# A four-layer GNN on one core: in the tensor product's edge stage, the eightfold copies of the hidden rows as one transfer each, the edge rows' products behind the next brackets, and TensorE's waits split by pair of chunks

## What is computed

```python
s1, v1 = scalars (16) and vectors (16 x 3) of both end nodes of an edge
w   = relu(emb @ fc1_w1 / sqrt(10)) @ fc1_w2 / sqrt(16)      # 4 matrices of 16 x 8 for each edge
s_t = a1 * (einsum(s1, Wss) + einsum(vdot1, Wvv))
v_t = a1 * (einsum(s1, Wsv) * sh1 + einsum(v1, Wvs))
w2  = relu(emb @ fc2_w1 / sqrt(10)) @ fc2_w2 / sqrt(16)      # 6 matrices of 8 x 8 for each edge
scal, gates, vecs = the same kind of products of s_t, v_t with w2
edge_out = concat([tanh(scal), vecs * tanh(gates)]) * norm
out = segment_sum(edge_out, edge_dst)
```

## Time and profile before

| what | us |
|---|---|
| time before, median of 3 runs | 26026.72 (26022.92 to 26029.44) |
| the profiled execution, its own time | 26033.88 |
| its span, first to last instruction | 26032.1 |
| DVE busy | 15740.5 (60%) |
| PE busy | 14761.0 (57%) |
| POOL busy | 14448.5 (56%) |
| ACT busy | 5279.9 (20%) |

### The profile page before, as it was taken

How to read it: one execution, slowest core, us unless ns; L and a number is a source line. 1 busy time by engine, 2 the same in 40 slices (tenths; PEclk the granted TensorE clock), 3 DMA queues, 4 the chain that set the end, 5 groups by cost and what they waited for, 6 DMA issues and landing times. The chain is left out here.

```text
span 26032.1 us, 473806 instructions
## 1 busy us (share of the span) xinstructions
PE 14761.0 (57%) x105565; PEld 9264.3 (36%) x105566; DVE 15740.5 (60%) x32221; ACT 5279.9 (20%) x13135; POOL 14448.5 (56%) x14298
## 2 busy tenths in 40 slices
PE   7555555567666679972000000005577777777777
PEld 5344444334333368851000000005233333333333
DVE  9666666665556654442111114995777777777777
ACT  4211111111111134421000000000222222222222
POOL 0377777677777744433777777760333333333333
PEclk9655555555555555555555555555899999999999
DMA  2466666533333345412333332221444544444454
GB/s 66 112 172 173 172 173 172 128 68 68 68 68 68 68 119 154 146 51 53 92 92 92 92 92 79 72 65 30 114 117 117 118 118 118 118 118 119 118 119 110
DMA packets 3004699, 2740.20 MB, mean 105 GB/s; under 512 B 1459983, under 2 KB 2366029, under 8 KB 3001618
## 3 DMA queue, kind: packets, MB, share of 16 engines
q1 hardware_dynamic: 2437198, 2308.99, 33.5%
q0 software_dynamic: 412544, 241.53, 6.4%
q10 hardware_dynamic: 153668, 172.93, 2.7%
HBM read 2173.27 MB, written 537.90 MB: 104 GB/s over the span
## 5 line engine op out<-in xcount | busy, mean ns | idle before, releaser
L2571 POOL DMA_INDIRECT rows_x<-x_table,index x3125 | 2961.4, 948 | 5359.1 <-DMA index<-in_src 4596.6
L742 POOL DMA_INDIRECT rows<-split_table,index x3125 | 2999.3, 960 | 1943.2 <-DMA index<-in_src 1008.4
L1624 POOL DMA_INDIRECT rows_dram<-rows,place_now x3125 | 3028.1, 969 | 1489.1 <-issue 951.9
L858 POOL DMA_INDIRECT rows<-x_table,index x3125 | 3282.0, 1050 | 1021.1 <-issue 951.8
L1552 DVE TENSOR_REDUCE rows<-banks 128x108 f32<-128x324 f32 x1250 | 490.3, 434 | 3468.9 <-DMA rows_dram<-rows,place_now 3452.6
L1564 PE MATMUL banks<-row_pieces,hot_turned 128*128 x3125 | 393.6, 290 | 3609.9 <-DMA hot_turned<-turned_dram 3606.6
L2278 DVE TENSOR_TENSOR first<-banks,h 128x768 f32<-128x768 f32 x2500 | 1940.0, 817 | 786.5 <-PE banks L2401 672.1
L2286 DVE TENSOR_TENSOR second<-banks,h 128x768 f32<-128x768 f32 x2500 | 1943.7, 819 | 620.1 <-PE banks L2425 604.1
L550 PE MATMUL banks<-counts,low_turned 128*128 128x98 f32 x6250 | 1783.2, 433 | 82.8 <-ACT counts L538 50.1
L550 PEld LDWEIGHTS banks<-counts,low_turned 128*128 128x128 f32 x6250 | 1591.6, 313 | 205.8 <-issue 175.9
L1564 PEld LDWEIGHTS banks<-row_pieces,hot_turned 128*128 128x128 bf16 x3125 | 251.0, 134 | 3752.5 <-issue 3752.5
(11 more groups left out here) (475 smaller groups left out, 33351.8 us busy)
## 6 DMA issues: line engine op xcount, KB each, us to landing
key_row<-dst_rows SPq DMA_DIRECT2D x1250, 320.0 KB, 3.5
h<-hidden_dram SPq DMA_DIRECT2D x10000, 40.0 KB
acc_moved<-dst_rows SPq DMA_DIRECT2D x625, 320.0 KB
src_row<-in_src_rows SPq DMA_DIRECT2D x625, 320.0 KB
hot_turned<-turned_dram SPq DMA_DIRECT2D x1250, 160.0 KB, 2.2
hot_dram<-onehot SPq DMA_DIRECT2D x625, 160.0 KB
turned_dram<-hot_turned SPq DMA_DIRECT2D x625, 160.0 KB
a_dram<-a ACTq DMA_DIRECT2D x625, 160.0 KB
```

Of the source, the lines that this page charges most:

```text
L742: nc.gpsimd.indirect_dma_start(out=m["rows"][j][:, t * SPLIT:(t + 1) * SPLIT], out_offset=None, in_=m["split_table"], in_offset=bass.Indir ...
L858: nc.gpsimd.indirect_dma_start(out=m["rows"][j][:, t * C2:t * C2 + F], out_offset=None, in_=m["x_table"], in_offset=bass.IndirectOffsetOnA ...
L1624: nc.gpsimd.indirect_dma_start(out=m["rows_dram"], out_offset=bass.IndirectOffsetOnAxis(ap=m["place_now"][j][:, t:t + 1], axis=0), in_=m[" ...
L2571: nc.gpsimd.indirect_dma_start(out=m["rows_x"][j][:, t * F:(t + 1) * F], out_offset=None, in_=m["x_table"], in_offset=bass.IndirectOffsetO ...
```

## The change

It has three parts. `sp_group` loads `h1` and `h2` with one transfer each, whose source repeats the 16 rows eight times (an outermost dimension of 8 with step 0). In `pe_turn` the brackets of the next group's half 0 move ahead of `pe_first_visit`. And in `pe_brackets`, `pe_units`, `pe_spread` and `pe_contract` the wait for VectorE's work moves into the loop over chunks: chunks 0 and 1 wait for the first of its two instructions, chunks 2 and 3 for the second.

```diff
--- before.py
+++ after.py
@@ -2192,10 +2192,9 @@
         if again:
             sp.wait_ge(s["doubled"], ONE + CHUNKS * (g - SLOTS + 1))
         for k, name in enumerate(("h1", "h2")):
-            for u in range(U8):
-                sp.dma_start(m[name][j][K16 * u:K16 * (u + 1), :],
-                             m["hidden_dram"][bass.ds(g, 1), K16 * k:K16 * (k + 1), :].rearrange("g h e -> (g h) e")
-                             ).then_inc(s["hidden_in"][j], 16)
+            sp.dma_start(m[name][j][:, :],
+                         m["hidden_dram"][bass.ds(g, 1), K16 * k:K16 * (k + 1), :].rearrange("g h e -> (g h) e").unsqueeze(0).broadcast_to([U8, K16, T * P])
+                         ).then_inc(s["hidden_in"][j], 16)
         if again:
             sp.wait_ge(s["hot_whole"], ONE + g - SLOTS + 1)
             sp.sem_inc(s["going_sp"], 1)
@@ -2272,7 +2271,7 @@
 
         width = HALVES[half][1]
         if half == 0:
-            dve.wait_ge(s["hidden_in"][j], 32 * U8 * (i + 1))
+            dve.wait_ge(s["hidden_in"][j], 32 * (i + 1))
         for pair in range(2):
             dve.wait_ge(s["brackets"], ONE + CHUNKS * (SLOTS * i + j) + 2 * half + pair + 1)
             nc.vector.tensor_tensor(m["first"][2 * half + pair][:, :].rearrange("p (k e) -> p k e", k=2), bank_pair(4 + 2 * pair, width),
@@ -2394,9 +2393,9 @@
     def pe_brackets(pe, i, j, half):
         g = SLOTS * i + j
         pe.wait_ge(s["flipped"], ONE + 2 * g + half + 1)
-        if not (isinstance(i, int) and g == 0):
-            pe.wait_ge(s["doubled"], ONE + CHUNKS * (g - 1) + 2 * half + 2)
         for chunk in range(CHUNKS):
+            if chunk % 2 == 0 and not (isinstance(i, int) and g == 0):
+                pe.wait_ge(s["doubled"], ONE + CHUNKS * (g - 1) + 2 * half + chunk // 2 + 1)
             rows = slice(32 * ((chunk - 1) % 4), 32 * ((chunk - 1) % 4) + 32)
             mm = nc.tensor.matmul(m["ps"][4 + chunk][:, 0:HALVES[half][1]], m["w_tensor"][rows, chunk * P:(chunk + 1) * P],
                                   m["u_turned"][j % 3][rows, columns(half)], start=True, stop=True)
@@ -2406,10 +2405,11 @@
     def pe_units(pe, i, j, half):
         g = SLOTS * i + j
         width = HALVES[half][1]
-        pe.wait_ge(s["weighted"], ONE + CHUNKS * g + 2 * half + 2)
         if not (isinstance(i, int) and g == 0):
             pe.wait_ge(s["outputs_out"], ONE + 2 * (g - 1) + half + 1)
         for chunk in range(CHUNKS):
+            if chunk % 2 == 0:
+                pe.wait_ge(s["weighted"], ONE + CHUNKS * g + 2 * half + chunk // 2 + 1)
             k = chunk % 2
             mm = nc.tensor.matmul(m["ps"][1][32 * chunk:32 * chunk + 32, 0:width], m["unit_sum"][:, :],
                                   m["first"][2 * half + chunk // 2][:, k * width:(k + 1) * width], start=True, stop=True)
@@ -2418,9 +2418,9 @@
     def pe_spread(pe, i, j, half):
         g = SLOTS * i + j
         pe.wait_ge(s["units_out"], ONE + 2 * g + half + 1)
-        if not (isinstance(i, int) and g == GROUPS - 1 and half == 1):
-            pe.wait_ge(s["weighted"], ONE + CHUNKS * g + 2 * half + 4)
         for chunk in range(CHUNKS):
+            if chunk % 2 == 0 and not (isinstance(i, int) and g == GROUPS - 1 and half == 1):
+                pe.wait_ge(s["weighted"], ONE + CHUNKS * g + 2 * half + chunk // 2 + 3)
             rows = slice(32 * chunk, 32 * chunk + 32)
             mm = nc.tensor.matmul(m["ps"][4 + chunk][:, 0:HALVES[half][1]], m["unit_spread"][rows, :], m["units"][half][rows, :],
                                   start=True, stop=True)
@@ -2429,13 +2429,14 @@
 
     def pe_contract(pe, i, j, half):
         g = SLOTS * i + j
-        pe.wait_ge(s["doubled"], ONE + CHUNKS * g + 2 * half + 2)
         if half == 0:
             pe.wait_ge(s["units_out"], ONE + 2 * g + 2)
         elif not (isinstance(i, int) and g == GROUPS - 1):
             pe.wait_ge(s["units_out"], ONE + 2 * g + 3)
         pe.wait_ge(s["outputs_out"], ONE + 2 * g + half)
         for chunk in range(CHUNKS):
+            if chunk % 2 == 0:
+                pe.wait_ge(s["doubled"], ONE + CHUNKS * g + 2 * half + chunk // 2 + 1)
             kind = min(chunk, 1)
             at_k = slice(chunk % 2 * T * P + HALVES[half][0], chunk % 2 * T * P + sum(HALVES[half]))
             mm = nc.tensor.matmul(m["ps"][1][32 * chunk:32 * chunk + 32, 0:HALVES[half][1]], m["w_second"][:, 32 * kind:32 * kind + 32],
@@ -2537,10 +2538,10 @@
             pe_units(pe, i, j, 1)
         if there(i, j, 2):
             pe_own(pe, *at(i, j, 2), first_ahead)
+        if there(i, j, 1):
+            pe_brackets(pe, *at(i, j, 1), 0)
         if there(i, j, -2):
             pe_first_visit(pe, *at(i, j, -2))
-        if there(i, j, 1):
-            pe_brackets(pe, *at(i, j, 1), 0)
         if there(i, j, 2):
             pe_own_further(pe, *at(i, j, 2), n_ahead)
```

## The result

The changed kernel takes 25401.6 us (median of four runs, 25380.8 to 25410.9) beside 26026.4 (26022.9 to 26029.4) of the kernel before: a ratio of 0.9759 with a 95% interval of 0.9743 to 0.9774, 625 us or 2.4% less. The forecast was 711 us less.

A forecast was written before the change was run, and what follows sets the result against it. SP's queue was taken to bound the last stage at 12.14 us a turn. SP's part (243 us) and the order and waits (468 us) make 711 us off the median of 26026.7, giving 25,315 us (25,150 to 25,500, chance 0.55).

The forecast's parts named there:

- SP is the pace: Last stage: SP's queue issues without waiting for buffers and sets the mean turn of 12.14 us.
- Rival three: SP's queue isn't the pace or isn't relieved: about 26,000 us, no change; chance 0.05.
- The gathers' cover: Indices issued on SP's queue: about 4 us of cover remain after the change, so late gathered rows drop out.
- SP's part alone: Two transfers for the hidden rows: mean turn falls from 12.14 to 11.75 us, 243 us in all; floor 0.
- The turn, 10.50 us: Undisturbed turn of TensorE and VectorE: 11.31 - 0.87 + 0.06 = 10.50 us.
- Undoing one alone gives nothing: Brackets ahead of `first`: second-instruction wait and products both hold them; only undoing both gains, 0.87 us a turn.
- The other pair waits: Split waits of `units`, `spread`, `contract` and half 1's brackets: give nothing; 0.63 us before `second` stays.
- The return: Loop's return every 15 turns: TensorE's stall met 0.87 us later, 0.40 us a turn; 0.10 more for small stalls.
- Two: TensorE's register load waits until the products are issued: mean turn 11.64, 25,715 us; 0.22 together with One and between.
- Four: New transfers run on half the DMA engines; if they pass the turn, 12.5 us a turn, 26,250 us; chance 0.05.
- One: Only SP's part comes, something else holds `first` at 11.31 us: 25,784 us; 0.22 together with Two and between.
- five: Better than forecast: a pair alone passes TensorE's array faster, mean turn 10.6 us, 25,065 us; chance 0.13.

The follow-up runs named there:

- e2_pe_only: Changed kernel with the hidden rows again in sixteen transfers, keeping the new order and pair waits: 25994.0 us, ratio 0.9999.
- e1_sp_only: Kernel before with only the hidden rows loaded by one transfer each, TensorE's order and waits as before: 25878.8 us, ratio 0.9955.
- e5_one_pair_wait: Changed kernel with the pair wait kept only for the brackets of half 0, whole waits elsewhere: 25420.9 us, ratio 0.9774.
- e4_old_order: Changed kernel with the edge rows' products ahead of the next brackets again: 25715.6 us, ratio 0.9893.
- e3_whole_waits: Changed kernel with TensorE's four waits ahead of the chunk loops again, for both VectorE instructions: 26051.8 us, ratio 1.0022.
- e8_no_rows_loaded: Changed kernel loading hidden rows only for the first five groups and reusing them (wrong values): 25277.7 us, ratio 0.9721.
- e6: Changed kernel with each hidden-row transfer reading 128 distinct rows of the first groups (wrong values): 25369.5 us, ratio 0.9753.
- e11: Changed kernel with partitions ordered hidden index first, copy second, so the source's outermost dimension is 16; right values: 25381.7 us, ratio 0.9766.

## Why the forecast came out as it did

**SP is the pace: right.** e2_pe_only leaves SP alone and gains nothing; SP's waits and its absence from the chain say the same. The gathers' cover was enough, as VectorE's two waits for them show. Rival three is out.

**SP's part alone, 243 us: measured 117 (75 to 161), by the two traces (12.14 - 11.90) x 624 = 150.** The mechanism was right, the size of one term wrong. The sum took the return as it was in one instance of before, 5.12 us. Its mean is 6.2, and it is no constant: it rises to 8.1 when 640 KB of hidden rows go out as two transfers. (8.1 - 5.12) x 40 = 119 us; the small stalls took 0.07 us a turn in place of the 0.10 left for them, which gives some 20 back. Together that is the difference by the traces. The rest of the way to 117 is in the baseline: the runs of before beside e1_sp_only had a median 31 us below the one that the forecast started from. The two transfers took SP 1.45 us with their gap and not 0.92 (timeline above), which costs nothing, since SP waits.

**The turn, 10.50 us: measured 10.33 to 10.37.** `second` to `first` came out as worked out, and the 0.06 us kept for `contract` and spread weren't needed. The two pairs take 1.69 us instead of 0.93, as the second starts 0.77 us behind the first, yet `first` starts 0.95 behind their start, with pair 0 done. The wait before `second` of half 0, which the forecast let stay, fell from 0.63 to 0.53 us, by the other pair waits (e5_one_pair_wait keeps 0.63 and e4_old_order has 0.53): 11.30 - 0.87 - 0.10 = 10.33. Ahead of the forecast by 0.14 x 624 = 87 us.

**"Undoing one alone gives nothing": right for the greater part of the gain, wrong for the time.** The changed kernel is 510 us below e1_sp_only, and neither edit gives that by itself: with the order alone the plain turn stays at 11.30, with the waits alone it is 11.12. But the waits alone are worth 161 us (e4_old_order), and the order alone costs 174 (e3_whole_waits). The forecast looked only at what holds `first`; it left out TensorE's clock, which fell with the new gap of 1.11 us, and the length of the branch.

**The other pair waits, nothing: right** within 0.15% (e5_one_pair_wait). They take 0.10 us from one wait and add 0.08 to the other.

**The return, (5.12 + 0.87) / 15 = 0.40 us a turn, with 0.10 for small stalls: measured 11.12 - 10.36 = 0.76.** This is the step that cost the most, 0.26 x 624 = 162 us. A return costs 9.8 us, and the turn behind it 0.75 more (11.11 on the mean). The parts, from differences between kernels: 6.2 as before; 1.9 for the burst of hidden rows (e1_sp_only less before; 2.6 by e8_no_rows_loaded); -1.3 with the pair waits (e4_old_order less e1_sp_only); and 3.0 with the new order (changed less e4_old_order), of which 0.87 was forecast. Of these 3.0 the branch has 1.2 (6.8 less 5.6). For the rest there is the clock: in the two turns of a return the changed kernel spends 12.0 us at 1.2 GHz and e4_old_order 8.2, and as the higher clock is twice the lower one, 3.8 us more of it are worth at most 1.9 where TensorE has no time to spare (an estimate). How the 3.0 divide between VectorE's earlier arrival, the branch and the clock was read from the traces, not isolated by an experiment.

The Trainium skill ("Runtime: NRT & Kernel Launch", section "Instruction fetch mechanics") says that a taken branch to code outside the fetched pages waits for a DMA of that code. The trace agrees: two instruction packets in every taken branch of before, the changed kernel, e1, e2 and e8, and 76 ns for the branch that isn't taken. What the hidden rows do to it is seen in the three pairs of kernels that differ in them alone: two large transfers in place of sixteen small ones make the branch 2.0 us longer (e1_sp_only less before) or 2.2 (changed less e2_pe_only), and leaving them out makes it 2.0 shorter (e8_no_rows_loaded). It isn't the mean traffic: e2_pe_only moves 119 GB/s and e8_no_rows_loaded 71, and their branches take 4.6 and 4.8 us. It is what fills the DMA engines during the branch: they are busy 0.30 of that time in e2_pe_only, 0.35 before, 0.64 in the changed kernel and 0.18 in e8_no_rows_loaded. The share alone isn't all of it: in e4_old_order it is 0.70, yet the branch takes 5.6 us, as its first packet often starts ahead of the branch.

**Rivals.** Two, a register load that isn't hidden, is false: `contract` follows the products without a gap, and TensorE's sequencer is at the load (0.31 us from 22005.19) while the products run. The Trainium skill's "TensorE: Matmul & The Clock Gate" (section "Architectural detail: the array is 16× 32×32, not 1× 128×128"), which the forecast cites, fits with its queue of 64; the reorder window that it names is for weight loads, and nothing here needed it. Four is true in its mechanism and false in its price: packets in flight and landings show fewer engines, but the load stayed under the turn, and 16 engines changed the time by 0.06% one way (e6) and 0.07% the other (e11), both within the noise. Its sum of 12.5 us a turn doesn't add up either: 8.9 with 0.8 x 5.3 more is 13.1. One and five didn't come; a pair alone takes 0.91 us where four chunks take 0.93, so that ground of five didn't hold. The result lies between the forecast and rival one, because of the return.

The sum by the measured terms: 711 forecast, + 87 for the turn, - 162 for the return, is 636, the stage's own difference; the medians give 625.

## What to carry to other kernels

A DMA queue that never waited for a buffer was the pace here, whatever the engines' busy shares said: look for its waits, count its issues per group, and expect relief elsewhere to be worth nothing until it waits. Splitting a wait and moving the work that filled it belonged together, and a gap on TensorE is to be priced with the turn behind it, where its clock may be halved. When turns get tight, price the loop's return from its mean over many rounds and ask what else uses the DMA engines at that moment; here longer bodies gave another 1.2 to 1.4%.

## What was not expected of the hardware

- The kernel with TensorE idle for 1.11 us ahead of the brackets (e3_whole_waits) spent 478 us of 4000 at 1.2 GHz away from returns; the one that differs from it in the order alone, with the products in that place, 17.
- The branch at the return depends on what the DMA engines do at that moment: 4.6 us with sixteen small transfers of the hidden rows (119 GB/s in the stage), 6.8 with two large ones (129), 4.8 with none (71). On the mean its first instruction packet starts 0.3, 2.2 and 0.6 us behind the branch's start.
- A 128-row load whose source repeats 16 rows costs SP 0.63 us to issue, beside 0.33 for the key row's of the same size, and at equal bytes 0.12 of the DMA engines' time more than the fixed 128 distinct rows of e6_all_engines.
- A pair of chunks on rows of the array of its own takes 0.91 us, four chunks sent together 0.93; a second pair that starts 0.77 us behind the first still takes its own 0.91.
